# Two jobs of VectorE handed to GpSimd in the last slot of a graph-convolution and LSTM kernel, and the last element normalised in three pieces

## The reference, cut to what matters

```python
def step(carry, x_t):                      # one step of a one-layer LSTM
    h, c = carry
    g = x_t @ Wih.T + h @ Whh.T + bias
    i, f, gg, o = jnp.split(g, 4, axis=-1)
    c = sigmoid(f) * c + sigmoid(i) * tanh(gg)
    h = sigmoid(o) * tanh(c)
    return ((h, c), None)

def _L1_gnn_ref(x, adj, Wg0, bg0, Wg1, bg1, Wih, Whh, bih, bhh):
    h = relu(einsum('ts,bsh->bth', adj, x @ Wg0 + bg0))
    h = relu(einsum('ts,bsh->bth', adj, h @ Wg1 + bg1))
    for p in range(1, 5):                  # LSTM of depth p over windows of p nodes
        nw = T // p
        last = lstm_last(Wih[p-1], Whh[p-1], bih[p-1], bhh[p-1],
                         h[:, :nw*p].reshape(B*nw, p, H))
        h = h.at[:, arange(nw)*p + p-1].set(last)
    return h

x = layernorm(x + L0_gnn(x, adj, adj, W1, W2, W3))     # three graph convolutions
x = layernorm(x + _L1_gnn_ref(x, adj, ...))            # x: 8 elements x 1024 nodes x 128 features
```

## Time and profile before

| | |
|---|---|
| median of 3 runs | 1012.63 us (1012.45 to 1013.11) |
| the profiled execution | 1012.88 us, of which its span 1011.2 us |
| busy in the span: TensorE, VectorE, ScalarE, GpSimd | 995.4, 560.3, 378.2, 19.9 us |
| the chain that ended last | TensorE 95%, VectorE 3%, ScalarE 1% |
| granted clock of TensorE | 0.9 or more in every slice but the last (0.8) |

### The profile page before, as it was taken

How to read it: one execution, slowest core, us unless ns; L and a number is a source line. 1 busy time by engine, 2 the same in 40 slices (tenths; PEclk the granted TensorE clock), 3 DMA queues, 4 the chain that set the end, 5 groups by cost and what they waited for, 6 DMA issues and landing times.

```text
span 1011.2 us, 14383 instructions
## 1 busy us (share of the span) xinstructions
PE 995.4 (98%) x5399; PEld 868.7 (86%) x5399; DVE 560.3 (55%) x1308; ACT 378.2 (37%) x702; POOL 19.9 (2%) x22
## 2 busy tenths in 40 slices
PE   9999999999999999999999999999999999999994
PEld 7888998888988889888898889898988989898894
DVE  7342343323334233332375656777777776767987
ACT  7231111222022120131234445445454464545765
POOL 0000000000000000000000000101010010100000
PEclk9999999999999999999999999999999999999998
DMA  9200000000000000000040000000000000000001
GB/s 358 95 1 1 1 1 1 1 1 1 1 0 0 0 0 0 0 0 0 0 166 1 1 1 1 1 1 2 22 1 21 0 21 0 21 2 22 1 1 64
DMA packets 7535, 20.42 MB, mean 20 GB/s; under 512 B 960, under 2 KB 2240, under 8 KB 7488
## 3 DMA queue, kind: packets, MB, share of 16 engines
q1 hardware_dynamic: 7488, 19.81, 5.2%
HBM read 15.61 MB, written 4.19 MB: 20 GB/s over the span
## 4 chain that ended last, share of the span: by engine, by line
PE 95%; DVE 3%; ACT 1%; issue 1%; DVEq 0%; ACTq 0%
PE ps L948 23%; PE ps L646 18%; PE ps L648 18%; PE ps L647 18%; PE ps L856 9%; PE ps L1001 2%; PE ps L1021 2%; PE ps L706 2%; PE ps L686 1%; PE ps L870 1%; PE ps L1063 1%; DVE stats L1323 1%; PE ps L1095 1%; PE ps L1064 0%; PE ps L1066 0%
## 5 line engine op out<-in xcount | busy, mean ns | idle before, releaser
L1306 DVE TENSOR_TENSOR y<-ps,y 128x512 fp32r<-128x512 f32 x46 | 31.8, 691 | 174.2 <-ACT y L1176 174.2
L1176 ACT ACTIVATE y<-ps 128x512 fp32r<-128x512 f32 x46 | 27.5, 598 | 269.3 <-PE ps L648 269.2
L646 PE MATMUL ps<-adj,node 128*128 128x512 f32 x312 | 122.2, 392 | 0.1
L648 PE MATMUL ps<-adj,node 128*128 128x512 f32 x312 | 121.7, 390 | 0.0
L647 PE MATMUL ps<-adj,node 128*128 128x512 f32 x312 | 121.6, 390 | 0.0
L646 PE MATMUL ps<-adj,h 128*128 128x512 f32 x256 | 99.7, 389 | 0.0
L647 PE MATMUL ps<-adj,h 128*128 128x512 f32 x256 | 99.7, 389 | 0.0
L648 PE MATMUL ps<-adj,h 128*128 128x512 f32 x256 | 99.6, 389 | 0.0
L1309 DVE SCALAR_TENSOR_TENSOR h<-ps,h 128x512 fp32r<-128x512 f32 x112 | 76.2, 688 | 40.0 <-ACT h L1176 39.4
L856 PE MATMUL ps<-s,adj 128*128 128x256 f32 x768 | 93.7, 283 | 0.0
L856 PEld LDWEIGHTS ps<-s,adj 128*128 128x128 f32 x768 | 92.9, 192 | 0.3
(11 more groups left out here) (214 smaller groups left out, 1690.2 us busy)
## 6 DMA issues: line engine op xcount, KB each, us to landing
square<-in_adj_t SPq DMA_DIRECT2D x8, 512.0 KB, 8.9
xb<-in_x SPq DMA_DIRECT2D x8, 512.0 KB, 11.0
adj_raw<-in_adj_t SPq DMA_DIRECT2D x8, 512.0 KB, 7.5
out<-xb SPq DMA_DIRECT2D x7, 512.0 KB, 2.7
lw_raw<-in_wih_t SPq DMA_DIRECT2D x1, 1024.0 KB, 12.4
lw_raw<-in_whh_t SPq DMA_DIRECT2D x1, 768.0 KB, 11.0
w_raw<-in_w SPq DMA_DIRECT2D x1, 512.0 KB, 11.6
out<-xb SPq DMA_DIRECT2D x1, 384.0 KB, 2.9
```

What stands on the lines that cost most here:

```text
L646: pe.matmul(dst, stat(HI), mov(HI), start=start, stop=False)
L648: return pe.matmul(dst, stat(LO), mov(HI), start=False, stop=stop)
L1176: nc.scalar.activation(dst, ps[:, (j * A_MM + q) % BANKS, :], func).then_inc(a_hi, 1)
L1306: nc.vector.tensor_tensor(dst, src, f32(hi), ALU.subtract).then_inc(done, 1)
```

## The change

Four things, all in the last slot (element numbers as above):

1. From the eighth step of the list on (Y31; `POOL_CELLS = 7`), the product i times g of every step with s > 0 is taken by GpSimd, in place, after it has waited for the gate g. VectorE waits for it before the sum. That is 12 products: 1 of 512 columns, 4 of 344, 7 of 258.
2. Element 5 is normed by GpSimd (`pool_scale`, 8 operations of 128x128) in place of ScalarE's shift (and VectorE's small L1740 for it).
3. The list is rearranged from Z41 on. The dummy matmuls before Z42 go (6 of them), those before Z43 are 3 in place of 7, and the input products of Z42 are issued ahead. The statistics of element 6 are split in two halves, the first before Z41.
4. Element 7 is added and measured in pieces: tiles 0 to 3 are added before Z43's sum, tiles 4 and 5 added and 0 and 1 measured between Z43's sum and its last product (Z43 is now held, ended by `("end",)`), then 2 to 5, then 6 and 7. At the end ScalarE norms three tiles, not two, and VectorE five, not six.

```diff
-                step(Y, 4, 3, back=2, held=True), ("stats", 3, 8, 3), step(Z, 4, 1), ("busy", 6), ("fin", 4, 8, 2),
+                step(Y, 4, 3, back=2, held=True), ("stats", 3, 8, 3), ("stats", 0, 4, 2), step(Z, 4, 1), ("ahead",),
...
+        POOL_CELLS = 7
+
+        def pool_cells(slot, k):
+            return slot == B and k >= POOL_CELLS and steps_of(slot)[k].s > 0
...
+                        if pool_cells(B, k):
+                            i, g = (gates_in(item.stream)[:, at, span(item)] for at in (GI, GG))
+                            pool.wait_ge(gate_act, AHEAD["gate"][B] + gate + 2)
+                            nc.gpsimd.tensor_tensor(i, i, g, ALU.mult).then_inc(pool_cell, 1)
...
+                elif item[0] == "pool_scale":
+                    _, t0, t1, back = item
+                    pool.wait_ge(ln_step, PAIRS * LN_STEPS + AHEAD["norm"][B] + n_norm)
+                    for t in range(t0, t1):
+                        g = norm_column(B - back) + t
+                        rows = xb[:, B - back, t, :]
+                        last = nc.gpsimd.tensor_scalar(rows, rows, mv[:, g, 0:1], newton[:, 1, g:g + 1],
+                                                       ALU.subtract, ALU.mult)
+                    last.then_inc(rows_ready(B, t0, t1, back), 1)
...
-                                nc.vector.tensor_tensor(work(GI), work(GI), work(GG), ALU.mult).then_inc(cell_step, 1)
+                                by_pool = pool_cells(slot, k_step)
+                                if not by_pool:
+                                    nc.vector.tensor_tensor(work(GI), work(GI), work(GG),
+                                                            ALU.mult).then_inc(cell_step, 1)
                                 dve.wait_ge(gate_act, ahead("gate", slot, turn, gate + 3))
                                 nc.vector.tensor_tensor(work(GF), work(GF), work(4), ALU.mult).then_inc(cell_step, 1)
-                                n_cell += 2
+                                n_cell += products(slot, k_step)
                                 step_reached(n_cell)
+                                if by_pool:
+                                    n_pool += 1
+                                    dve.wait_ge(pool_cell, n_pool)
                                 nc.vector.tensor_tensor(work(4), work(GI), work(GF), ALU.add).then_inc(cell_done, 1)
```

More of the change, by code:

```diff
@@ L344, in build @@
                 step(Y, 4, 2, back=2, held=True), step(Z, 4, 0), ("fin", 0, 4, 2), ("ahead",),
[L345 to L348 removed]
+                step(Y, 4, 3, back=2, held=True), ("stats", 3, 8, 3), ("stats", 0, 4, 2), step(Z, 4, 1), ("ahead",),
+                ("fin", 4, 8, 2), ("stats", 4, 8, 2), step(Z, 4, 2), ("root2", 0, 8, 2), ("ahead",),
+                ("fin", 0, 4, 1), ("busy", 3), step(Z, 4, 3, held=True), ("fin", 4, 6, 1), ("stats", 0, 2, 1),
+                ("end",), ("shift", 0, 8, 2), ("pool_scale", 0, 8, 3), ("stats", 2, 6, 1), ("fin", 6, 8, 1),
+                ("stats", 6, 8, 1), ("root", 0, 8, 1), ("shift", 5, 8, 1), ("scale", 0, 5, 1)]
+        POOL_ADDS = ()
         SLOTS = B + 1
@@ L368, in parts_of @@
         def parts_of(e):
-            return sum(not isinstance(item, Step) and item[0] in ("scale", "shift") and slot - item[3] == e
+            return sum(not isinstance(item, Step) and item[0] in ("scale", "shift", "pool_scale") and slot - item[3] == e
                        for slot, full in ((B - 1, DRAIN), (B, LAST)) for item in full)
@@ L378, in norm_column, with pool_adds, adds_so_far @@
             return NORM_COLUMN.get(e, 0)
+        def pool_adds(slot, item):
+            return slot == B and item[1:] in POOL_ADDS
+        def adds_so_far(slot, n_fin):
+            first = [item for item in items(slot) if item[0] == "fin"][:n_fin]
+            by_pool = sum(pool_adds(slot, item) for item in first)
+            return by_pool, n_fin - by_pool
         def items(slot):
@@ L393, in items @@
                 else:
-                    back = item[-1] if item[0] in ("fin", "stats", "root", "root2", "scale", "shift") else 0
+                    back = item[-1] if item[0] in ("fin", "stats", "root", "root2", "scale", "shift", "pool_scale") else 0
                 if slot < back:
@@ L414, in ends, with products, cell_steps @@
             return u.p == SKIPS and u.s == SKIPS - 1
-        def cell_steps(u):
-            return (2 if u.s > 0 else 0) + (0 if ends(u) else 2)
+        POOL_CELLS = 7
+        def pool_cells(slot, k):
+            return slot == B and k >= POOL_CELLS and steps_of(slot)[k].s > 0
+        def products(slot, k):
+            return 0 if steps_of(slot)[k].s == 0 else 1 if pool_cells(slot, k) else 2
+        def cell_steps(slot, k):
+            return products(slot, k) + (0 if ends(steps_of(slot)[k]) else 2)
         def high_counts(slot):
             n, begun, counts = 0, [], []
-            for u in steps_of(slot):
-                n += 2 if u.s > 0 else 0
+            for k, u in enumerate(steps_of(slot)):
+                n += products(slot, k)
                 for v in finished_by(u, begun):
@@ L434, in build @@
             "unit": lambda n: len(steps_of(n)),
-            "cell": lambda n: sum(cell_steps(u) for u in steps_of(n)),
+            "cell": lambda n: sum(cell_steps(n, k) for k in range(len(steps_of(n)))),
             "fin": lambda n: count(n, "fin"),
@@ L627, in _, with first_half_of_runs @@
             back = 1
-            for slot in range(back, SLOTS):
+            def first_half_of_runs(slot):
                 steps = steps_of(slot)
@@ L1563, in hi_ready @@
                     dve.wait_ge(b_hi, ahead("lo", slot, turn, B_PRE + n))
[L1565 removed]
+                gate, n_cell, n_fin, n_norm, begun, n_ended, k_step, n_pool = 0, 0, 0, 0, [], 0, 0, 0
                 def in_place(u, g):
```

48 lines of the change are left out of this document (45 added, 3 removed).

## The result

The changed kernel takes 1017.03 us (median of 7 runs, 1016.3 to 1017.43); the kernel before, on the same chip, 1012.99. The ratio is 1.0040, with a 95% interval of 1.0031 to 1.0049: 4.0 us slower. The forecast was 1013.8, with a range up to 1016.5: the measured time lies 0.5 us above the range. One of the seven runs of the kernel before took 3529 us; neither its median nor the ratio rests on it. The profiled execution spans 1015.7 us (before: 1011.2). Its GpSimd copy of the last slot, ahead of every changed instruction, already starts 0.52 us later than before (944.58 against 944.06); that much belongs to the execution, not to the change, and the last column leaves it out.

What follows compares the result with a forecast made beforehand. The prediction took TensorE to bound the kernel to 975 us, VectorE's round nearly as long, and VectorE's queue the tail from 984 us. Middle +1.5 and tail -0.4 gave +1.1, so 1013.8 us, range 1011.0 to 1016.5.

Steps and rivals of the forecast that it cites:

- VectorE stands still beside a product: Last slot: VectorE's operations on SBUF wait until GpSimd has finished, then need only their stream of columns.
- rival B: VectorE is not held beside a GpSimd product; middle -0.3, total -1.3, 1011.3 us; chance 0.22.
- Duration d: Time of one product on GpSimd: taken as 0.58, 0.78 and 1.16 us for 258, 344 and 512 columns.
- The middle, +1.5: Y31 to Y42: eight products on GpSimd lengthen VectorE's rounds, 0.30 + 0.84 + 0.36 = +1.5 us.
- Tail products, -0.54: From 984 us: Y43's product about 0, Z41's and Z42's together -0.66, Z43's +0.12; together -0.54 us.
- Pieces +0.48: Tail, VectorE: three more statistics groups +0.45, an addition cut in two +0.13, a small shift gone about -0.1.
- tanh -0.48: Tail: VectorE's 0.48 us idle during Z43's tanh is filled by an addition and two tiles' statistics.
- end -0.05: From the root's end to the second output issue: 1.85 us in place of 1.9.
- GpSimd's norm, +0.2: Tail: eight operations at 0.29 us last 2.3 us, hold Z43's last product and the shift once each, end before `root`.
- Rival D: TensorE's clock falls to 1.2 GHz before Z42's or Z43's gates: +1.0 on the forecast, 1014.8 us; chance 0.04.
- Rival C: GpSimd reads one input after the other, twice the copy's time: middle 4.7, tail about 0, 1017.3 us; chance 0.24.
- The sum: Whole change: middle +1.5 and tail -0.4 give +1.1 us.

Runs made afterwards that it cites:

- shadow: Kernel before, VectorE multiplying everything itself, plus twelve same-size GpSimd products on other data nobody waits for: 1018.65 us, ratio 1.0059.
- cells_three: Rearranged list with only the last three products (Z41, Z42, Z43) on GpSimd, element 5 normed by ScalarE: 1012.37 us, ratio 0.9994.
- order_alone: Changed kernel with only the rearranged list left: neither products nor the norm of element 5 on GpSimd; 1012.43 us, ratio 0.9995.
- three_busy: order_busy with the last three products (Z41, Z42, Z43) on GpSimd: 1013.47 us, ratio 1.0006.
- order_busy: order_alone with eight dummy matmuls before Z42's input products and eight in place of three before Z43: 1013.68 us, ratio 1.0007.
- norm_early: cells_back with GpSimd's eight norm operations of element 5 right behind step Z43 in the list: 1012.51 us, ratio 0.9996.
- norm_back: Changed kernel with element 5 normed by ScalarE again, right behind step Z43, products still on GpSimd: 1014.63 us, ratio 1.0016.
- out5_later: Changed kernel with element 5's output issued by SyncE between the two parts of element 7: 1016.10 us, ratio 1.0031.
- cells_back: Changed kernel with all products i times g back on VectorE, the norm of element 5 still on GpSimd: 1015.06 us, ratio 1.0021.
- cells_left_out: Changed kernel with the twelve products i times g done by neither engine, and no wait for them: 1014.09 us, ratio 1.0010.
- changed_norm_early: Changed kernel with GpSimd's eight norm operations of element 5 right behind step Z43 in the list: 1014.61 us, ratio 1.0016.
- norm_half: cells_back with GpSimd norming only tiles 0 to 3 of element 5 and ScalarE tiles 4 to 7: 1012.34 us, ratio 0.9994.

## Why the prediction was wrong

- **VectorE stands still beside a product** (rival B's opposite): right. shadow shows it with products nobody waits for, and Z32's f times c ends 0.38 us behind GpSimd, where 0.39 was forecast.
- **Duration d**: too short. Taken 0.58, 0.78 and 1.16 us for 258, 344 and 512 columns, measured 0.74, 0.93 and 1.29. The nearest row, a copy-like operation of 128 columns with one input, was no good guide; the upper bounds held. The Trainium skill's table for the GPSIMD engine (GPSIMD Engine Reference, Performance versus the Vector engine), scaled to 344 columns, gave an estimate of 0.76 us; the trace has 0.93, so neither the row nor the scaled page had the size.
- **The middle, +1.5**: mis-sized by this. With the measured durations the same formula gives 0.43 + 4 x 0.36 + 3 x 0.28 = +2.7; the high part of Y42's h is 2.2 later, and the runs price all products at 2.0 to 2.4. The form was right and somewhat too strict; perhaps not every round was without slack, which no run tested.
- **Tail products, -0.54**: not confirmed. Only Z41's product lay wholly beside statistics. Y43's and Z42's held f times c to 0.64 us, and Z43's held the last operation of `root2` to 0.64, where 0.17 is usual. cells_three is 0.06 under order_alone, three_busy 0.21 under order_busy, and neither can be told from 0. Taking a microsecond off VectorE's queue there was not worth a microsecond: even all twelve for nothing brought 1.0.
- **Pieces +0.48, tanh -0.48, end -0.05**: the sum of about 0 against -0.6 measured, with an interval that holds both. Each of them alone wasn't tried.
- **GpSimd's norm, +0.2: the step that failed.** "GpSimd's eight norm operations at 0.29 us last 2.3 us" and "they end before `root`". They last 6.35 us, 0.79 each, and end 1.1 us behind the root. Even my "at 0.45 each +0.5" bounded it too low, by a row of another kind of operation; I drew no upper bound at all. Yet the duration alone isn't the loss: norm_early has 6.51 us and pays nothing. What I didn't ask is who waits for the last of the eight. SyncE's queue is in order, with element 5's output first; the end of the prediction followed ScalarE's and VectorE's tiles to the last two issues and took it that the two ahead of them were gone. That is 2.4 us (changed kernel less norm_back), of which out5_later recovers 0.9 by the order of issues alone.
- **Rival D**: in the changed kernel the granted clock is 1.00 in every 2 us up to 1004, so its case didn't arise there; it arose in order_alone, for at most 0.1 us. Its reading of the kernel before left out the transposes of Z43, which kept TensorE at work until 1001.03. **Rival C** had nearly the right time, 1017.3, for the wrong reason: it put +4.7 on the middle, where 2.2 came, and nothing on the end.
- **The range** took the uncertainty of d on the products, but none on the norm, which used the same row; an error of a factor of 2.7 in that term was outside it.
- **The sum**: +1.1 was forecast and 4.0 measured. The norm is 2.2 of the difference, the products (+1.5 - 0.54 against 2.0 to 2.4) 1.0 to 1.4, and the list takes 0.6 back, which was luck.

## What to carry over

An operation moved to an idle engine has two prices: what it does to the engine beside it while it runs, and who waits for its end. For the second, follow the in-order queue of output issues: one tile that is ready late holds back the finished ones behind it, and their transfers then stand in a row at the end, where nothing hides them. Before offloading from a nearly full engine that doesn't set the end, leave the work out in one run: here that gave 1.0 us for 4.7 us of VectorE's time, half of what the products cost on GpSimd.

## What the runs showed of the hardware

- GpSimd's norm of a tile (128 x 128, two scalars per partition) takes 0.79 us, about as long as a product of 258 columns with two tile inputs (0.74), and 2.7 times the 0.29 us of the one-input operation of the same size.
- Of VectorE's root operations on 8 columns beside GpSimd's norm only some are held, at most 0.38 us in place of 0.17, while beside a product f times c and the low part of h stand still until it ends (they end 0.29 to 0.66 us behind it), and so does the one high part that started during a product (0.76 us in place of 0.34, at 966.81).
- A GpSimd product is itself held at times: 1.10 us for 344 columns at 960.36, where 0.93 is usual, while VectorE's high part of h ran until 960.68; and 1.80 for 512 in shadow, behind i times g, where 1.29 is usual.
- The issue of the two last outputs takes 2.02 us when two others were issued right before them (the changed kernel, cells_back, cells_left_out), and 0.82 to 0.84 where 0.8 us or more lie between (norm_back, norm_early, changed_norm_early, norm_half).
